# Late routing divided between the engines, and the end of attention reordered, in an adaLN block of linear attention and a routed feed-forward layer

## The reference

```python
h = _layernorm(x) * (1 + ca) + sa
x = x + ga * attention(h)            # q, k = relu(hWq), relu(hWk); v = hWv;
                                     # s = gamma*s + k v^T, z = gamma*z + k; y = q s / (q z)
h = _layernorm(x) * (1 + cb) + sb
logits = h @ Wr.T + br               # 8 experts
expert = argmax(logits, -1)          # one expert for each token
x = x + gb * (relu(h @ W1[expert].T + b1[expert]) @ W2[expert].T + b2[expert])
```

## Time and profile before

| | |
|---|---|
| median of the runs | 463.11 us (463.03 to 463.56) |
| profiled execution | 461.84 us |
| its span, first to last instruction | 459.7 us |
| attention's last score to first output of the feed-forward layer | 204 to 231 us |
| feed-forward tiles with the late routing beside them | 231 to 269 us |
| the rest of the feed-forward layer | 269 to 452 us |

### The profile page before, as it was taken

One profiled execution on the slowest core, in us unless ns is written; L12 is line 12 of the kernel. 1 busy time (PEld: TensorE's weight loads), 2 busy tenths in 40 slices (PEclk: granted clock), 3 DMA queues, 4 the chain that ended last, 5 costly groups with the idle time before them and its releaser, 6 DMA issues.

```text
span 459.7 us, 14510 instructions
## 1 busy us (share of the span) xinstructions
PE 423.1 (92%) x4704; PEld 383.4 (83%) x4704; DVE 382.4 (83%) x1026; ACT 333.0 (72%) x844; POOL 266.8 (58%) x432
## 2 busy tenths in 40 slices
PE   7999899999999899876698499999999999999993
PEld 4988789888898788764597399999999999999992
DVE  2978999999999998987789968787877777888863
ACT  1557889999999788843778457777777777777770
POOL 2032567767777687667674347666655665565332
PEclk9999999999999999999699989999999999999998
DMA  8725354555655374122131023221212222100000
GB/s 288 247 93 166 133 163 161 163 161 165 180 176 165 135 250 140 35 75 89 46 113 41 12 60 97 60 77 56 72 50 72 69 66 63 51 25 26 20 18 2
DMA packets 23448, 46.91 MB, mean 102 GB/s; under 512 B 4683, under 2 KB 17228, under 8 KB 21200
## 3 DMA queue, kind: packets, MB, share of 16 engines
q1 hardware_dynamic: 17424, 31.82, 21.3%
q0 software_dynamic: 4992, 12.60, 9.1%
q10 hardware_dynamic: 960, 1.57, 1.0%
HBM read 35.22 MB, written 13.50 MB: 106 GB/s over the span
## 4 chain that ended last, share of the span: by engine, by line
PE 75%; DVE 12%; issue 5%; POOL 3%; DMA 2%; ACT 2%; DVEq 0%; POOLq 0%; ACTq 0%
PE ps_o L1857 20%; PE ps_qk L1831 11%; PE ps_va L1831 10%; PE ps_qk L1727 8%; PE ps_o L1682 5%; PE ps_kv L1689 5%; PE ps_va L1736 4%; PE ps_va L1710 3%; PE ps_o L1678 2%; DMA w<-in_wmod 2%; PE ps_k L1700 1%; PE ps_x L1592 1%; DVE arena L1424 1%; DVE w L1438 1%; PE ps_x L1796 1%
## 5 line engine op out<-in xcount | busy, mean ns | idle before, releaser
L1857 PE MATMUL ps_o<-w,arena 128*128 x912 | 105.9, 273 | 0.0
L1857 PEld LDWEIGHTS ps_o<-w,arena 128*128 128x128 f16 x912 | 87.5, 98 | 9.8 <-issue 0.4
L1438 DVE COPY w<-w 128x2048 f16 x78 | 60.5, 776 | 31.2 <-PE ps_qk L1831 24.8
L830 ACT ACTIVATE arena<-ps_qk,arena 128x128 f32<-128x128 f32 x156 | 44.6, 369 | 55.5 <-PE ps_qk L1831 52.6
L1831 PE MATMUL ps_qk<-arena,w 128*128 128x128 f16 x936 | 61.7, 225 | 7.4 <-DVE arena L1477 3.7
L1831 PEld LDWEIGHTS ps_qk<-arena,w 128*128 128x128 f16 x936 | 58.0, 101 | 9.5 <-issue 4.5
L680 POOL DMA_INDIRECT out_rows<-arena,slot_token x39 | 45.8, 1175 | 33.7 <-POOL arena L674 30.6
L1831 PE MATMUL ps_va<-arena,w 128*128 128x128 f16 x936 | 60.2, 222 | 1.8 <-DVE w L1438 1.8
L1424 DVE TENSOR_TENSOR arena<-arena 128x512 f16<-128x512 f32 x78 | 53.7, 688 | 8.2 <-ACT arena L838 8.2
L674 POOL TENSOR_TENSOR arena<-arena 128x256 f32<-128x256 f32 x38 | 29.1, 767 | 53.0 <-DVE arena L1528 53.0
L1831 PEld LDWEIGHTS ps_va<-arena,w 128*128 128x128 f16 x936 | 57.0, 100 | 2.6 <-DVE w L1438 2.1
(11 more groups left out here) (268 smaller groups left out, 871.9 us busy)
## 6 DMA issues: line engine op xcount, KB each, us to landing
w<-in_w_raw SPq DMA_DIRECT2D x16, 1024.0 KB, 5.4
token_rows<-arena SPq DMA_DIRECT2D x64, 128.0 KB, 2.8
arena<-in_x SPq DMA_DIRECT2D x32, 128.0 KB, 2.2
b_sb<-in_b2b SPq DMA_DIRECT2D x1, 1024.0 KB, 5.3
w<-in_wmod ACTq DMA_DIRECT2D x1, 768.0 KB, 8.2
w<-in_wqkv SPq DMA_DIRECT2D x1, 768.0 KB, 8.0
arena<-token_rows,slot_token POOLq DMA_INDIRECT x39, 3.5
out_rows<-arena,slot_token POOLq DMA_INDIRECT x39, 2.6
```

The costliest lines, as they stand in the source:

```text
L830: last = act.activation(hid[:, f, :], bank[("qk", "va")[h]][:, (f % 4) * P:(f % 4 + 1) * P], ACT.Relu, bias=consts_now[:, r, f:f + 1], sca ...
L1438: dve.tensor_copy(now[:, :, i * F // 2:(i + 1) * F // 2], of[:, :, i * F // 2:(i + 1) * F // 2]).then_inc(s_w1, 1)
L1857: last = pe.matmul(bank[f"o{n % 2}"][:, 0:D], hid_parts[:, r % 2, b, f, :], w[:, bass.ds(m, 1), a, f * D:(f + 1) * D].rearrange("p a d -> ...
```

## The change

It has four parts. **Logits**: GpSimd computes the logits of two tiles in two instructions right behind their deviations (`second_deviations`), and VectorE's L1316 is gone. **End of attention**: GpSimd's slots stop at k = 16; deviations of tiles 28 and 29 come before the first gathers, those of 30 and 31 right behind the tile constants, and the modulations of tiles 28 to 31 are put between later gathers. ScalarE does the last matrix's pieces before the norms of tiles 28 and 29, and those of 30 and 31 and the copy of gate_b's rows (`last_norms`) inside tile 0. VectorE does two pieces of matrix 14 before x1 of tile 30. TensorE transposes tiles 1 to 3 in other places. Gates are made one tile later. **Late routing**: the add and the product that end `late_places` go to GpSimd (between its gather for tile 8 and its sum for tile 1), and late_slots waits for them; marks are divided 16 on VectorE, 8 on GpSimd, 8 on ScalarE. **Numbers**: `matrix_number(n + 1)` is read after the copies of tile n, not before the first copy. Buffers move: `place` and `upto` have places of their own, the gate has two buffers.

```diff
-DVE_MARKS = 24
+DVE_MARKS, POOL_MARKS = 16, 8
@@ GpSimd @@
+            def second_deviations(j):
+                need(pool, s_xn2, 2 * j - 2)
+                inverse_deviations(j, s_mv2, mv2, rs2, s_rs2s, s_rs2)
+                if j == 0:
+                    pool.wait_ge(s_setup_read, 1)
+                q, these = j % 2, logits[:, B * j:B * j + B, :]
+                pool.tensor_tensor(these, x1_sb[:, :, q, D:DX], rs2[:, q, :, 1:2].to_broadcast([P, B, NE]),
+                                   ALU.mult).then_inc(s_lgm, 1)
+                pool.wait_ge(s_lgm, j + 1)
+                pool.tensor_tensor(these, these, logit_c[:], ALU.add).then_inc(s_lgr, B)
...
             slots(pool, *ATT, slot)
 
+            second_deviations(NCH // B - 2)
+            first_gathers()
+            tile_constants()
+            second_deviations(NCH // B - 1)
+            constants_of(0)
+            pool.wait_ge(s_x1, NCH - 1)
+            gather(2)
+            constants_of(1)
+            pool.wait_ge(s_x1, NCH)
+            gather(3)
+            constants_of(2)
+            modulate(NCH - 4, 0, NCH // B - 2)
+            pool.wait_ge(s_o, NCH)
+            gather(4)
+            constants_of(3)
+            modulate(NCH - 3, 1, NCH // B - 2)
+            modulate(NCH - 2, 0, NCH // B - 1)
+            modulate(NCH - 1, 1, NCH // B - 1)
+            constants_of(4)
             for b in range(B):
                 pool.wait_ge(s_sx[b], 16 * (NCH // B))
                 pool.wait_ge(s_sh[b], 16 * (NCH // B))
-            pool.wait_ge(s_lgr, NCH)
-            for n in range(4, 6):
-                gather(n)
-                constants_of(n)
+            gather(5)
+            constants_of(5)
...
+                if s == TA - 7:
+                    pool.wait_ge(s_first, 1)
+                    pool.tensor_tensor(of_experts(place), of_experts(place), by_expert(first, NCH),
+                                       ALU.add).then_inc(s_placed, 1)
+                    pool.wait_ge(s_placed, 1)
+                    pool.tensor_tensor(place, place, chosen16, ALU.mult).then_inc(s_placed, 1)
+                if s in (TA - 6, TA - 4):
+                    pool.wait_ge(s_minus, 1)
+                    i = (s - TA + 6) // 2
+                    for n in range(i * MARKS, (i + 1) * MARKS):
+                        last = pool.tensor_scalar(in_slot[:, DVE_MARKS + n, :], slot_no16, slot_of_pool[:, n:n + 1], None,
+                                                  ALU.is_equal)
+                    last.then_inc(s_pool_bits, 1)
@@ ScalarE @@
             slots(act, *ATT, slot)
 
-            act.wait_ge(s_gbrow, 1)
-            act.activation(gate_b, bank["o0"].rearrange("p (b d) -> p b d", b=B), ACT.Copy).then_inc(s_gb_sb, 1)
+            second_norm(NCH - 4, NCH // B - 2, 0)
+            second_norm(NCH - 3, NCH // B - 2, 1)
+            token_hi(0, 0)
...
+                    if it[0] == 0:
+                        last_norms()
+                    early_gate(it[0])
@@ VectorE @@
+                if (k, u) == (FULL, 0):
+                    lo_piece(k, u, 0)
+                    lo_piece(k, u, 1)
                 if attend:
...
-                    dve.wait_ge(s_rs2s, 3 * (n // B) + 2)
-                    dve.scalar_tensor_tensor(logits[:, n, :], x1_sb[:, r, g % 2, D:DX], rs2[:, g % 2, r, 1:2],
-                                             logit_c[:, r, :], ALU.mult, ALU.add).then_inc(s_lgr, 1)
...
-                hop(dve.scalar_tensor_tensor(of_experts(place), by_expert(first, NCH), float(P), of_experts(place),
-                                             ALU.mult, ALU.add))
-                dve.wait_ge(s_chosen, 2)
-                dve.wait_ge(s_removed, 1)
-                mark(dve.tensor_tensor(place, place, chosen16, ALU.mult))
+                dve.tensor_scalar(first, first, float(P), None, ALU.mult).then_inc(s_first, 1)
 
             def late_slots():
-                level()
+                dve.wait_ge(s_placed, 2)
+                dve.wait_ge(s_h2, NCH)
...
+                if (it := ffn_item(k, u, 0)) and it[0] == TA - 4:
+                    mark_slots(in_slot, slot_f, 3)
                 if (it := ffn_item(k, u, -1)) and it[0] > 0:
                     alone(dve, (s_hp, 2 * it[0] - 1))
-                    m = matrix_number(it[0])
+                    m = matrix_of[it[0]]
                     copy_w1(m, it[0], 0)
-                    whole_gate(it[0])
+                    if it[0] == 1:
+                        token_lo(1, 1)
                     if cur := ffn_item(k, u, 0):
                         hidden_lo(cur[0], cur[2], 0)
                     copy_w1(m, it[0], 1)
+                    if it[0] + 1 < NT:
+                        matrix_number(it[0] + 1)
...
+                    whole_gate(n)
...
-                    if n in (2, 3, 4):
-                        for i in ((0, 1), (2, 3), (4, 5))[n - 2]:
+                    if n in (2, 3):
+                        for i in ((0,), (1, 2))[n - 2]:
                             mark_slots(in_slot, slot_f, i)
@@ TensorE @@
-                    if n == DVE_MARKS:
+                    if n == DVE_MARKS + POOL_MARKS:
                         pe.wait_ge(s_act_bits, 1)
+                    elif n in (DVE_MARKS, DVE_MARKS + MARKS):
+                        pe.wait_ge(s_pool_bits, (n - DVE_MARKS) // MARKS + 1)
...
-                        if i == 0 and n == 0:
-                            transpose_tokens(1, 0, 1)
-                        elif (i == 0 or n == 0) and (ahead := ffn_item(k, u, -AHEAD)):
+                        if n < 2:
+                            if (n, i) != (0, 1):
+                                transpose_tokens(n + i + 1, 0, n + i + 1)
+                        elif i == 0 and (ahead := ffn_item(k, u, -AHEAD)):
                             transpose_tokens(*ahead)
                     if n == 0:
                         late_ranks()
+                    if n == 1:
                         pe.wait_ge(s_gb_sb, 1)
```

115 lines of the change are left out of this document (57 added, 58 removed).

## The result

The changed kernel takes 457.76 us in the median of 4 executions (456.91 to 459.13), beside 463.33 us for the kernel before (463.03 to 463.56): a ratio of 0.9883, 95% interval 0.9857 to 0.9909, which is 5.4 us (4.2 to 6.6). The forecast was 457.0. The profiled execution of the changed kernel took 457.60 us, its span is 455.8.

What follows compares the result with a forecast made beforehand. TensorE is busy throughout 269.4 to 440.5 us, so only earlier time can be gained; the second half waits for GpSimd's queue. 4.1 + 2.0 = 6.1 us, 463.11 - 6.1 = 457.0 us, range 451.0 to 461.3.

Steps and rivals of the forecast that it cites:

- Attention, forecast 2.0 us: In attention, moving the logits from VectorE to GpSimd gains 2.0 us, ends -2.3 and +3.9.
- I count half: In attention at 145 to 206 us, half of the 3.9 us of L1316 taken off VectorE counts as gain: 2.0 us.
- The slower rival, by the shared port: Added GpSimd instructions hold up VectorE: 2.3 us lost in attention, 4.2 on the chain behind it; 465.5 us, chance 0.09.
- The wait for the places: After attention, late_slots on VectorE waits about 6.4 us for GpSimd's place operations and starts at 241.9 us.
- The table: Durations added in queue order from attention's end, attention unshifted: places end at 241.9 us, tile 9 transposed at 269.1.
- The rival of the places not being late: VectorE need not wait for the places: late_slots at 235.5, tile 9 at 263.2; 451 us, chance 0.20.
- The late part, forecast 4.1 us: Behind attention, tile 9 is transposed at 269.1 us instead of 273.2, 4.1 us earlier.
- The port: GpSimd's code product L667 falls on VectorE's work for tile 4's slot and costs it 1.0 us, 0 to 2.
- The marks: In late routing, each of GpSimd's eight 128x128 marks takes 0.4 us, ends 0.2 and 0.9.
- I cost it at nothing: TensorE's clock falling after idling before tile 4 and the last marks: 1.2 us more per group, counted as 0.
- A difference carries over: The 6.1 us gain, worked out on a profiled execution of 461.84 us, is subtracted from the median of 463.11.
- The rule of the shared port: GpSimd shares SBUF interfaces with VectorE and contends with its instructions that have two SBUF inputs.

Runs made afterwards that it cites:

- The undone part: The changed kernel with the logits computed on VectorE again, all else as changed: 460.15 us, ratio 0.9923.
- the part alone: The kernel before with nothing changed but the logits moved to GpSimd: 459.54 us, ratio 0.9913.

## Why the prediction was right, and where its steps failed

The time came out 0.8 us from the forecast, and the direction and the main events are as forecast. But two terms were wrong by more than that, in opposite directions.

**Attention, forecast 2.0 us, measured 3.05.** The step "I count half" of L1316's 3.9 us was too small: of 10 instructions in the last 60 us alone 3.9 us come off VectorE's queue, and TensorE got 3.05 back over the whole of attention. The undone part moves the projection back to 200.08, the part alone brings it to 196.35, so the term is the logits' and nothing else's. The slower rival, by the shared port, is out: the two instructions cost 0.57 us a pair and VectorE is busy for less time.

**The wait for the places, forecast and found.** The table put their end at 241.9 us with attention unshifted. The kernel with the logits back on VectorE has attention unshifted and all the rest of the change, and there VectorE goes on at 241.93:

```profile
241.93 0.59 DVE L1418 TENSOR_REDUCE pick<-arena 128x32 f32<-128x256 f32 x1 [5.41 <-POOL arena L683]
```

For the changed kernel, shifted by the measured 3.05 us, that is 238.85; VectorE goes on at 239.38. That it fits so well is in part luck, since in both kernels steps on the way are off and cancel: gather 5 starts late, at 230.79 us (229.6 in the table) and at 228.75 (226.6 shifted), and the gathers behind it are shorter than the table's 1.9 us. The hole before tile 4 came, 3.2 us long instead of 5.6: tile 2's output ahead of it ended at 238.45 us where the shifted forecast has 235.8, because tile 0's output first waited 2.18 us for ScalarE (222.95) and took 4.46 us instead of 2.78. The first down projection is at 222.95 us (222 to 225 forecast), gather 9 at 263.83 (263 to 266), and the steady stage is full. The rival of the places not being late is what the kernel with the places on VectorE shows: 455.0 to 456.7 us, not 451, because the numbers were next.

**The late part, forecast 4.1 us, measured 0.9.** At the last number product, ahead of any question of the clock, it is 1.2 us where 4.5 was forecast (it ends at 260.93 us instead of 265.19, less the 3.05). With the forecast's times shifted by 3.05 us:

| step | forecast, shifted | measured |
|---|---|---|
| late_slots starts | 238.9 | 239.38 |
| GpSimd's second four marks end | 257.0 | 260.39 |
| last number product ends | 257.5 | 260.93 |
| gather 9 starts | 262.4 | 263.83 |
| tile 9 transposed | 266.1 | 269.23 |

Three terms make the 3.4 us by which GpSimd's second marks end late. The chain to the places gave 0.5. The port gave 1.1: the copy lost 2.1 us (2.81 less 0.69), where 1.0 was taken and 2 was the end of the bounds; moving the product away gives the copy back. The marks gave 1.5: 0.78 us each in the second four where 0.4 was taken from a two-input row, inside the ends of 0.2 and 0.9. The first four cost nothing, since GpSimd then waits 2.96 us for VectorE. What is left, 0.3, is spread over the outputs. In the kernel with the logits back the same steps, unshifted, are late by about as much: the last number product ends at 263.50 us (260.5 forecast), tile 9 is at 272.35 (269.1).

The step "I cost it at nothing" for the clock failed with them. It held only while gather 9 was the last to come. Three stretches of the changed kernel, the wait for the numbers, the groups behind it, and the end of tile 6 (length, busy us and count of PE, PEld, DVE, ACT, POOL, then the granted clock):

```profile
257.00:260.40 3.40, 0.00 (x0) 0.00 (x0) 3.29 (x7) 0.00 (x0) 3.35 (x5) 1.00 0.11 39
260.50:264.50 4.00, 4.00 (x49) 3.94 (x50) 2.85 (x12) 0.97 (x4) 2.52 (x3) 0.57 0.12 39
265.00:269.20 4.20, 4.20 (x56) 3.92 (x54) 3.35 (x7) 2.77 (x8) 2.99 (x4) 1.00 0.40 110
```

After 3.4 us without a product TensorE works for most of 4 us at the lower of its two levels (0.57 in the mean, where 0.5 is 1.2 GHz), and then again at 2.4 GHz. The groups take 2.72 and 1.73 us instead of 1.50 each, 1.45 us in all, and nothing covered them: with gather 9 at 263.83 and a landing after 3.4 us tile 9 could have been transposed near 267.3, and TensorE reached it at 269.23 without waiting. In the kernel with the second marks early these groups run at 1.50 us, and the gather is the bound, as the forecast had it.

**The base of the sum.** "A difference carries over" was wrong by about 1.4 us. The traces give 3.98 us, the times of the two profiled executions 4.2, the medians 5.6 (5.4 by the ratio). The profiled execution of before, 461.84 us, lies under each of the others shown with it (463.03 to 463.56) and under all later ones (462.01 to 464.37); that of the changed kernel lies inside its own. The trace of before has a candidate. From its last number product to tile 9 it takes 8.02 us, and with the logits alone moved, behind a wait as long, 9.27, with the same work in between: the second group runs at the higher level in the one and at the lower in the other (1.50 and 2.69 us). In the other kernels that waited as long for the last marks it is 8.2 to 8.9 us. If the kernel before usually takes the longer time, a typical pair of traces would show a gain of up to 5.2 us instead of 4.0; with one profiled execution of it that is not shown. So the forecast of 6.1 us stands against 4.0 us between the two traces and 5.4 us of measured gain. It erred by 1.1 us too little in attention and by 3.2 too much behind it, and its nearness to the measured gain is in part luck.

**The edits within the change.** By these runs: the logits bring 4.0 us by themselves (by the ratio) and 1.9 on top of the rest; reading the number ahead about 1 us, within the noise; dividing the marks 1 to 2 us; moving the places to GpSimd loses 1.6 us in the medians and 2.6 in the trace; putting the second marks a turn too late in GpSimd's queue loses 1.8 us in the medians (456.00 against 457.76) and 0.5 in the trace. The reordering at the end of attention wasn't tried by itself, so its share is open.

**The rule of the shared port.** VectorE's copy of 128x2048 f16 has one input and was held just as long as the two-input instruction of the earlier trace rows: 2.81 us, its own 0.69 and the product's 1.80 one after the other, and 0.3 more. The Trainium skill (SBUF — State Buffer, "SBUF: two separate sides") says that the pair of ports which VectorE and GpSimd share is locked for a whole instruction, so that the other is blocked fully, and that VectorE needs it for instructions in a two-port mode too, not only for those with two SBUF inputs. The rows agree with it: a copy with one input was held. The prediction had named the narrower half of that rule, and had taken half of a collision where it comes whole.

## What to carry to other kernels

Before work goes to an idler engine, add up what stands ahead of it in that engine's queue and who waits for its result: the logits were free on GpSimd because nobody waited for them there, the two place operations (0.4 us each on VectorE) cost 2.6 us because a wait for a store, four gathers, a sum and a scatter stood ahead of them. When a chain has several waits one behind another, each repair shows only what the next wait leaves of it, so measure them together too. And put early in a queue whatever the bounding engine asks for, before making it faster. Of long elementwise work on GpSimd beside VectorE, count the whole collision (here 2.1 us for an operation of 1.8).

## What was not expected of the hardware

- GpSimd's comparison of 128x128 f16 with one value a partition takes 0.59 to 0.64 us with VectorE idle and up to 1.19 us beside it in the changed kernel, where a two-input f32 operation of that size took 0.45.
- The same four marks on GpSimd took 3.30, 3.86, 4.88, 5.51 and 5.86 us in kernels that differ in what VectorE does beside them; VectorE's batch of marks took 0.68 or 1.78 us. Their work is the same in all.
- The length of one wait doesn't tell whether TensorE's granted clock falls behind it: after 3.18 us of idle the next group took 1.50 us at 1.00 in the changed kernel (241.63); after 4.44 us it took 2.72 at 0.50 in the kernel that reads the number late, and after only 2.59 us also 2.72 at 0.50 in the one with the late product on VectorE.
